# Start of a four-layer graph network on one core: the edge list is loaded first and alone, the clearing of the sums begins earlier, and later layers' weights are scaled inside layer 0

## The reference

```python
h = act(edge_scalars @ fcW1) @ fcW2                  # 192 weights per edge
msg = products(h, (x @ W1)[src], edge_attr)          # 64 + 32 scalars, (64 + 32) x 3 vectors
agg = segment_sum(msg, dst, num_segments=n)
x = layernorm(x + gate_sc * (x @ W_sc) + gate_c * (agg @ W2))
```

## Time and profile before

| | before |
|---|---|
| median of 3 runs | 3560.47 us (3559.24 to 3563.49) |
| profiled execution, its own time | 3561.85 us |
| its span | 3560.1 us |
| busy in the span | PE 84%, DVE 78%, ACT 71%, POOL 67% |
| layer 0, edge part, POOL's first to last scatter | 123 to 621 us |
| TensorE clock granted, mean | 0.957 of full speed |

### The profile page before, as it was taken

The page is one execution under the profiler, slowest core; times in us unless marked ns, Lnnn a source line. Parts: engine busy times, 40 slices in busy tenths (PEclk is TensorE's granted clock), DMA queues, the critical chain, the costliest instruction groups (busy, mean ns, idle before and its releaser), DMA issues. The chain is left out here.

```text
span 3560.1 us, 90904 instructions
## 1 busy us (share of the span) xinstructions
PE 3003.0 (84%) x21186; PEld 2686.6 (75%) x21186; DVE 2759.2 (78%) x9716; ACT 2521.2 (71%) x7974; POOL 2379.9 (67%) x2641
## 2 busy tenths in 40 slices
PE   2777777676669999899979998999979999978887
PEld 1677767565659999777768887777778888877776
DVE  2577776788868888688878887788868888868887
ACT  0466665566657777577779887677778888858888
POOL 1477776788867777777767777700057777757776
PEclk9899999888889999899999999899999999989999
DMA  8622222777742222599942223799922222237776
GB/s 347 232 55 61 63 65 78 231 258 249 253 133 54 60 63 65 189 319 299 298 126 57 63 65 81 239 305 297 293 64 50 56 59 60 63 132 256 257 257 225
DMA packets 424056, 567.55 MB, mean 159 GB/s; under 512 B 218798, under 2 KB 242380, under 8 KB 420486
## 3 DMA queue, kind: packets, MB, share of 16 engines
q1 hardware_dynamic: 295142, 317.19, 30.5%
q0 software_dynamic: 81680, 114.98, 12.2%
q10 hardware_dynamic: 47088, 133.90, 9.5%
HBM read 349.68 MB, written 233.74 MB: 164 GB/s over the span
## 5 line engine op out<-in xcount | busy, mean ns | idle before, releaser
L1044 ACT ACTIVATE arena<-bank,meta 128x96 f32<-128x96 f32 x3136 | 767.5, 356 | 123.5 <-PE bank L863 55.5
L1320 DVE TENSOR_TENSOR_SCAN arena<-wide,arena,bank 128x256 f32<-128x256 f32 (+1 forms) x1164 | 782.3, 727 | 65.4 <-PE bank L832 60.0
L581 POOL DMA_INDIRECT xg<-x_after,meta_all x588 | 592.8, 1008 | 251.6 <-issue 168.4
L1117 ACT ACTIVATE arena<-arena,shift,rstd 128x160 f32<-128x160 f32 x1600 | 697.4, 508 | 65.8 <-DVE shift L1397 63.8
L590 POOL DMA_INDIRECT aggregates<-arena,meta_all x392 | 396.4, 1011 | 190.5 <-issue 95.2
L1471 DVE BATCH_NORM_STATS2 stats<-arena 128x6 f32<-128x160 f32 x1600 | 453.4, 313 | 41.0 <-DVE arena L1464 7.5
L590 POOL DMA_INDIRECT aggregates<-wide,meta_all x392 | 394.0, 1005 | 119.5 <-issue 95.7
L1091 ACT ACTIVATE nT<-bank 128x640 f32<-128x640 f32 x400 | 279.5, 699 | 245.6 <-PE bank L942 160.0
L822 PE MATMUL bank<-ident,xg 128*128 128x128 f32 x1176 | 208.5, 287 | 252.6 <-DMA xg<-x_after,meta_all 108.9
L942 PEld LDWEIGHTS bank<-sc_cols,nT 128*128 128x128 f32 x2400 | 331.0, 205 | 86.4 <-issue 86.4
L822 PEld LDWEIGHTS bank<-ident,xg 128*128 128x128 f32 x1176 | 133.6, 144 | 292.4 <-issue 174.0
(11 more groups left out here) (177 smaller groups left out, 7152.8 us busy)
## 6 DMA issues: line engine op xcount, KB each, us to landing
arena<-aggregates SPq DMA_DIRECT2D x400, 324.0 KB
x_after<-arena ACTq DMA_DIRECT2D x300, 320.0 KB
arena<-x_after SPq DMA_DIRECT2D x300, 320.0 KB
aggregates<-arena ACTq DMA_DIRECT2D x25, 1296.0 KB, 15.3
arena<-nodes SPq DMA_DIRECT2D x100, 320.0 KB
out<-arena SPq DMA_DIRECT2D x100, 320.0 KB
xg<-x_after,meta_all POOLq DMA_INDIRECT x588
wide<-run_flags SPq DMA_DIRECT2D x7, 896.0 KB, 11.9
```

What stands on the lines that cost most here:

```text
L581: gp.indirect_dma_start(xg[:, q % XGR, 4 + t * F:4 + (t + 1) * F], None, xtab[l], at).then_inc(gathered[q % RING], 16)
L1044: last = nc.scalar.activation(wy[:, k1 % 2, t, h, :], bank[2][:, w_at:w_at + 96], ACT.Copy, scale=meta[:, k1, y_at + 4 * t + h:y_at + 4 * ...
L1117: last = nc.scalar.activation(row, row, ACT.Identity, bias=shift[:, kk, t:t + 1], scale=rstd[:, kk, t:t + 1])
L1320: last = nc.vector.tensor_tensor_scan(aggT[:, slot, c, :], flags_all[:, bass.ds(row, 2 * P)], turned_msg, before, ALU.mult, ALU.add)
```

## The change

- The list is loaded once, as `pairs1` with `prev1` and `next1`, straight from the inputs, and nothing else is issued ahead of it. The check and the fields are made from it. Only the sorting branch loads it again.
- `sorted_pairs` and `sorted_first` are not copied any more (the sorting branch fills them). `sorted_attr` is still copied, in two parts (the first 14 pairs, then the rest), after the list has landed.
- On ACT the small weights go first and wait for the list; the large array `main` waits for the first four attributes (`attr_in0`); the clearing runs come right behind it and wait for `blank` alone.
- The fills of `blank`, `xg` and `l2_rows` move from DVE to POOL.
- DVE scales only layer 0's edge weights in the preparation; those of layers 1, 2 and 3 are scaled at the head of steps 8, 9 and 10 of layer 0 (6, 8 and 10 instructions), and PE waits for them ahead of layer 1. PE turns the four small matrices earlier. The columns that PE reads of the small weights are named by `L2_AT`.

```diff
@@ SP
-            sp.dma_start(pairs0, pair_rows(pairs)).then_inc(given_in, 16)
+            sp.dma_start(pairs1, pair_rows(pairs)).then_inc(list_in, 16)
             sp.wait_ge(filled, 1)
-            sp.dma_start(prev0[1:NPAIR, :], pair_rows(pairs)[0:NPAIR - 1, 510:512]).then_inc(given_in, 16)
-
-            sp.wait_ge(records_ready, 1)
-            sp.wait_ge(rows_blank, 1)
-            sp.dma_start(pairs1, pair_rows(rec_pairs)).then_inc(rows_in, 16)
...
+            sp.dma_start(prev1[1:NPAIR, :], pair_rows(pairs)[0:NPAIR - 1, 510:512]).then_inc(list_in, 16)
+            sp.dma_start(next1[0:NPAIR - 1, :], pair_rows(pairs)[1:NPAIR, 0:2]).then_inc(list_in, 16)
+            sp.dma_start(attr_rows, pair_rows(first4)).then_inc(attr_in0, 16)
+
+            sp.wait_ge(flags_made, 1)
...
                 if l == 0:
                     sp.wait_ge(meta_ready, 1)
-                    sp.wait_ge(attr_moved, 16)
+                    sp.wait_ge(attr_moved_first, 16)
@@ POOL
-            gp.dma_start(rec_pairs.rearrange("(q e) c -> q (e c)", q=P), pairs.rearrange("(q e) c -> q (e c)", q=P)).then_inc(copied, 16)
-            gp.dma_start(rec_first4.rearrange("(q e) c -> q (e c)", q=P), first4.rearrange("(q e) c -> q (e c)", q=P)).then_inc(copied, 16)
-            gp.dma_start(rec_attr.rearrange("(q e) c -> q (e c)", q=P), eattr.rearrange("(q e) c -> q (e c)", q=P)).then_inc(attr_moved, 16)
-            gp.wait_ge(copied, 32)
+            gp.memset(blank, 0.0).then_inc(blank_ready, 1)
+            gp.memset(xg[:, :, :], 0.0).then_inc(blank_ready, 1)
+            gp.wait_ge(list_in, 48)
+            for first, n, moved in ((0, FIRST_ATTRS * 2, attr_moved_first), (FIRST_ATTRS * 2, NT - FIRST_ATTRS * 2, attr_moved)):
+                rows = slice(first * P, (first + n) * P)
+                gp.dma_start(rec_attr[rows, :].rearrange("(q e) c -> q (e c)", q=P), eattr[rows, :].rearrange("(q e) c -> q (e c)", q=P)).then_inc(moved, 16)
...
+            gp.wait_ge(fields_ready, 1)
+            gp.memset(l2_rows, 0.0).then_inc(l2_blank, 1)
             gp.wait_ge(meta_ready, 1)
@@ ACT
-            act.dma_start(weights[:, :], main).then_inc(weights_in, 16)
+            act.wait_ge(list_in, 48)
             act.dma_start(raw, small).then_inc(weights_in, 16)
+            act.wait_ge(attr_in0, 16)
+            act.dma_start(weights[:, :], main).then_inc(main_in, 16)
             act.wait_ge(blank_ready, 1)
...
-            act.wait_ge(rows_in, 48)
             for run in range(Z_FIRST):
@@ DVE
-            dve.wait_ge(given_in, 32)
-            nc.vector.tensor_copy(dst0, pairs0.rearrange("q (e c) -> q e c", c=2)[:, :, 1])
...
+            dve.wait_ge(list_in, 48)
+            turn_fields(link)
+            link(nc.vector.tensor_tensor(less0, dst1, prv1, ALU.is_lt))
             nc.vector.tensor_reduce(viol, less0, AX.X, ALU.max).then_inc(viol_ready, 1)
+            compare_fields(link)
...
+                    if l == 0 and isinstance(q, int) and 8 <= q < 11:
+                        last = scale_edge_weights(q - 7)
+                        if q == 10:
+                            last.then_inc(later_scaled, 1)
```

More of the change, by code:

```diff
@@ L448, in edge_loads @@
                         wait(sp, turned, edge_count(l, q - XGR))
+                        if l == 0 and isinstance(q, int) and q == FIRST_ATTRS:
+                            sp.wait_ge(attr_moved, 16)
                         alone(sp, passed["sp"])
@@ L763, in _ @@
             for t in range(2):
-                last = nc.tensor.transpose(bank[1][:, t * NPAIR:(t + 1) * NPAIR], dst0[:, t * P:(t + 1) * P],
+                last = nc.tensor.transpose(bank[1][:, t * NPAIR:(t + 1) * NPAIR], dst1[:, t * P:(t + 1) * P],
                                            ident[0:NPAIR, 0:NPAIR])
             last.then_inc(cols_turned, 1)
+            o = L2_AT
+            pe.wait_ge(weights_in, 16)
+            for j in range(4):
+                last = nc.tensor.transpose(bank[6][0:96, 96 * j:96 * j + 96], raw[0:96, o + 96 * j:o + 96 * j + 96],
+                                           ident[0:96, 0:96])
+            last.then_inc(l2_done, 1)
             pe.wait_ge(fields_ready, 1)
@@ L780, in _ @@
             nc.tensor.transpose(bank[0][0:1, P:P + NPAIR], run1[:, 255:256], ident[0:NPAIR, 0:NPAIR]).then_inc(counts_turned, 1)
-            o = L2_AT
-            pe.wait_ge(weights_in, 32)
-            for j in range(4):
-                last = nc.tensor.transpose(bank[6][0:96, 96 * j:96 * j + 96], raw[0:96, o + 96 * j:o + 96 * j + 96],
-                                           ident[0:96, 0:96])
-            last.then_inc(l2_done, 1)
             pe.wait_ge(l2_copied, 1)
@@ L1132, in link, with turn_fields, compare_fields @@
                 dve.wait_ge(chain, count[0])
-            link(nc.vector.memset(prev0, -1))
+            two = lambda ap: ap.rearrange("q (e c) -> q e c", c=2)
+            def turn_fields(done):
+                nc.vector.tensor_copy(dst1, two(pairs1)[:, :, 1])
+                nc.vector.tensor_copy(src1, two(pairs1)[:, :, 0])
+                nc.vector.tensor_copy(nxt1, next1[:, 1:2])
+                nc.vector.tensor_copy(prv1[:, 0:1], prev1[:, 1:2])
+                done(nc.vector.tensor_copy(prv1[:, 1:256], two(pairs1)[:, 0:255, 1]))
+            def compare_fields(done):
+                done(nc.vector.tensor_tensor(same1, dst1, prv1, ALU.is_equal))
+                nc.vector.tensor_copy(flag1, same1)
+                nc.vector.tensor_copy(later1[:, 0:255], same1[:, 1:256])
+                done(nc.vector.tensor_tensor(later1[:, 255:256], dst1[:, 255:256], nxt1, ALU.is_equal))
+                done(nc.vector.scalar_tensor_tensor(out=idx1, in0=later1, scalar=FAR, in1=dst1, op0=ALU.mult, op1=ALU.add))
+            nc.vector.memset(prev1, -1)
+            link(nc.vector.memset(next1, -1))
             dve.engine_nop().then_inc(filled, 1)
-            nc.vector.memset(blank, 0.0).then_inc(blank_ready, 1)
             nc.vector.memset(ones[:, :], 1.0)
@@ L1195, in _, with again @@
                     nc.vector.tensor_copy(sort_s[:, 8:9].bitcast(i32), rank).then_inc(pos_ready, 1)
[L1196 to L1217 removed]
+                    then(nc.vector.tensor_scalar(edge, edge, float(P), None, ALU.add), t * per + (per + 3))
+                dve.engine_nop().then_inc(pos_ready, 1)
+                dve.wait_ge(resorted, 64)
+                chained = [NT * per + 3]
+                def again(ins):
+                    chained[0] += 1
+                    ins.then_inc(sort_chain, 1)
+                    dve.wait_ge(sort_chain, chained[0])
+                turn_fields(again)
+                compare_fields(again)
+            dve.wait_ge(records_ready, 1)
+            dve.engine_nop().then_inc(flags_made, 1)
             dve.engine_nop().then_inc(fields_ready, 1)
```

103 lines of the change are left out of this document (45 added, 58 removed).

## The result

| | before | after |
|---|---|---|
| median | 3561.91 us (6 runs, 3559.24 to 3565.63) | 3546.05 us (6 runs, 3541.48 to 3548.85) |
| ratio | | 0.9954, interval 0.9943 to 0.9964 |
| profiled execution, its own time | 3561.85 us | 3542.26 us |
| its span, mean granted clock | 3560.1 us, 0.957 | 3540.6 us, 0.962 |
| POOL's first scatter | 123.02 us | 111.44 us |

The change gained 15.9 us (12.8 to 20.3 by the interval).

What follows compares the result with a forecast made beforehand. POOL, held until the last clearing run lands behind full DMA engines, was taken to bound layer 0's edge part. 25.0 - 12.8 - 2.25 - 0.4 = 9.5 us off 3560.5 gave 3551.0 us, range 3547 to 3558.

Steps and rivals of the forecast that it cites:

- main term: Layer 0's edge part: the last clearing run's landing releases POOL, so the full DMA window slides with its start, 25.0 us earlier.
- Start 25.0 us earlier: Clearing on ACT's queue: `main` issued and DMA engines full from 6.3 us instead of 31.3; bounds 5.5 and 8.0.
- 5.21 MB of copy and `main`, 12.8 us: Clearing window: net traffic added by the `sorted_attr` copy and `main`, less the first attributes' load; 12.8 us back at 407 GB/s.
- One more flag piece, 2.25 us back: SP's queue in the clearing window: earlier pairs bring one more 0.92 MB run-flag piece, costing 2.25 us; bounds 0 and 6.75.
- `small` ahead of the window: Small weights' load (0.59 MB) should be through before `main` starts; if not, 1.5 us more.
- POOL beside DVE's scaling, 0.4 us back: Layer 0's steps 8 to 10: DVE's 3.0 us of scaling lengthens POOL's issues, costing 0.4 us; bounds 0 and 3.0.
- Rival D: Layer 0's steps 8 to 10: POOL pays for the scaling in full, gain 6.9 us, 3553.6 us; chance 0.08.
- Cover: Preparation: earlier list check, fields, `meta_ready` and POOL's fills gain or cost nothing, because POOL can't pass `zeroed` before the clearing ends.
- Pair 0 at PE between 45 and 57: Sign that the forecast is right: layer 0's first pair reaches PE at 45 to 57 us, estimated about 49.
- rival E: Clearing starves: if pair 0 comes late, DMA engines fall idle before the last run; slower, for example 3570 us; chance 0.06.
- Any change from layer 1 on, where nothing differs: Sign that the forecast is wrong: layers 1 and later, whose program is the same, should show no change.
- C: Clearing window: start at 8.0 (-1.7), `small` inside (-1.5), three flag pieces (-4.5); any two give 3554 to 3557; chance 0.17.

Runs made afterwards that it cites:

- n_flags_act: Changed kernel with the six later flag pieces issued on ACT's queue behind the ninth clearing run instead of on SP's: 3561.0 us, ratio 1.0003 to before.

## Why the prediction was wrong, point by point

The mechanism of the main term held: POOL is released by the last clearing run, the window of full DMA engines slides with the clearing's start, and the preparation is covered. Its sum was 25.0 - 12.8 - 2.25 - 0.4 = 9.5 us.

The issue of flag piece 1 on SP, on which one term hangs, in before:

```profile
101.80 5.61 SPq L429 DMA_DIRECT2D wide<-run_flags  x1
```

And in after:

```profile
82.87 5.64 SPq L421 DMA_DIRECT2D wide<-run_flags  x1
```

- **Start 25.0 us earlier:** 24.8 (6.53 against 31.32). The list was read at 4.58 (forecast 4.5).
- **5.21 MB of copy and `main`, 12.8 us:** right; taking the copy out moved the first scatter by 9.5 us for 3.81 MB (9.4 at 407 GB/s), by which the copy is priced.
- **One more flag piece, 2.25 us back: the first step that failed.** The price is about right (2.7 us by n_flags_act), but the count is not: 1.9 pieces lie in the window, 0.2 fewer than before and not one more. The pairs came as I had worked out (pair 0 at PE at 48.65, its total done at 93.67), and so one more piece was issued in the window. But I took the issue for the traffic. Piece 1 (rows above) was issued at 101.80 in before and at 82.87 in after. Its data began to move at 116.23 in before, 6.8 us ahead of the first scatter, and at 108.56 in after, 2.9 ahead, 25.7 us behind its issue: until then SP's queue moved the packets of 128 bytes and less of the pairs' loads, which stood ahead of it. With 1.08 MB less on SP's queue than I had summed (2.34 MB against 2.90 - 0.40 + 0.92) this is worth 2.6 us.
- **`small` ahead of the window:** 0.53 MB of it lay inside, 1.3 us the other way. My bound had it at 1.5.
- **POOL beside DVE's scaling, 0.4 us back:** nothing. In steps 8 to 10 POOL's issues took 0.96 to 1.02 us with 0.30 between them, as in the earlier trace rows, and taking the scaling out changed nothing. The 1.25 of the earlier trace rows was not due to the scaling, or not to it alone. Rival D falls; by the rule of the Trainium skill, page "SBUF — State Buffer", section "Who interferes with whom", it would have been 3.0 us. The rule itself is not refuted, for it looks as if DVE was the one that waited: six of the 24 instructions took 0.35 to 0.45 us instead of 0.16 to 0.24, and all six started under an issue of POOL and ended within 0.1 us of its end (others that started under one took no longer). That is the 3.5 us instead of 3.0, and DVE had room for it. No run isolates what they waited for.
- **Cover:** "Pair 0 at PE between 45 and 57": 48.65; `meta_ready` near 16.6. POOL's fill of `blank` took 2.25 us, as DVE's had. There was no hole before the last run (the DMA share averages 1.07 from 6 to 16 us, is 0.78 to 0.95 from 16 to 24, and 1.0 and more from there to 108), so rival E did not come; even with the fields 14 us later only 4 us were lost.
- **"Any change from layer 1 on, where nothing differs" was to show me wrong: the second step that failed.** 2.0 to 2.7 us of the gain lie in layer 3's node part, from two stalls that the place of DVE's code makes. Nothing in my rows could have priced it, but the profile of before had the 0.23 us gaps.
- **The range:** its upper end was mis-summed. Two thirds of C's 7.7 us leave 4.4 us of the gain, 3556 and not 3558. The miss was at the other end.

First scatter 11.6 us earlier instead of 9.9; no charge on POOL, 12.1 at the last pair; 2.0 to 2.7 from the place of the code: 14.1 to 14.8 us, against a forecast of 9.5. The medians gave 15.9 (12.8 to 20.3) and on another chip 13.3 (ratio's interval 9 to 18.5). The profiled execution's 19.6 us hold 4.0 more by TensorE's clock, which other executions have and lack alike. What stays open is whether the change moves the moment of such a stretch in the mean, and what makes the two stalls at some places of the code.

## What to carry to other kernels

Where full DMA engines set the end of a phase, count the bytes between its first and last transfer, queue by queue, and ask for each transfer whether it must lie there: putting off 4.7 MB brought 9 us more than the change had. What its queue holds ahead of a transfer can decide whether it is in the window: piece 1 was issued 28.6 us ahead of the first scatter and moved nothing until 2.9 us ahead of it. And a gain of a few us in stages that the edit doesn't touch should be looked for block by block before it is called noise: moving code can make or mend stalls in a loop far behind it, and a handful of empty instructions shows it.

## What the runs showed of the hardware that I had not expected

- Seven places in DVE's program decide over two stalls of 0.10 and 0.13 us per turn of a loop of 210 instructions. The Trainium skill, page "Runtime: NRT & Kernel Launch", section "Instruction fetch mechanics", says that fetching is hidden by the time that each instruction takes to issue, except where a taken branch leaves the two blocks held. No run here shows that the stalls are waits for instructions. If they are, this case's trace doesn't agree: the one of 0.13 us lies in the fifth of the turn's eight blocks, where no branch is taken.
- The same program takes 4246 and 4286 us on two chips and 3559 to 3562 in the three comparisons on others. The extra time is not everywhere: in the kernel before, layer 2's node part takes 3.313 us per block on both kinds of chip, layer 1's 3.32 and 4.69, layer 0's edge part 5.19 and 6.60 per pair. What differs in these chips no run here shows.
- DMA issues on SP that took 0.5 us each before the clearing filled the engines took up to 6.2 us each in it.
